# State-space stage of a four-layer kernel: spread products placed in opposite row halves of TensorE, sines stored 64 rows off, products of constants in front of three waits

## The reference, cut to what matters

```python
def _rope(t, theta):
    na = theta.shape[-1]                      # 32 angles
    x1, x2, rest = (t[..., :na], t[..., na:2 * na], t[..., 2 * na:])
    c, s = (jnp.cos(theta), jnp.sin(theta))
    return jnp.concatenate([x1 * c - x2 * s, x1 * s + x2 * c, rest], axis=-1)
...
theta = jnp.cumsum(angles[:, :, None, :] * dt[..., None], axis=1)
Bn = _rmsnorm(Bg, B_norm_w)
Cn = _rmsnorm(Cg, C_norm_w)
K = _rope(Bn[:, :, None, :] + B_bias, theta)
Q = _rope(Cn[:, :, None, :] + C_bias, theta)
...
S1 = jnp.einsum('bcihn,bcjhn->bcijh', Qc, Kc) * g1c[:, :, None, :, :] * decay
...
y = (y_intra + y_inter).reshape(b, L, NHEADS, HEADDIM)
y = y + D[None, None, :, None] * x
y = y * jax.nn.silu(z)
return y.reshape(b, L, D_INNER) @ W_out
```

## Time and profile before

| | us |
|---|---|
| median of 3 runs | 2860.07 |
| lowest and highest | 2855.85, 2862.87 |
| the profiled execution's own time | 2858.35 |
| its span, first to last instruction | 2856.4 |
| PE busy in the span | 2418.9 |
| DVE busy | 2147.7 |
| ACT busy | 1681.9 |
| POOL busy | 1036.5 |

### The profile page before, as it was taken

How to read it: one execution, slowest core, us unless ns; L and a number is a source line. 1 busy time by engine, 2 the same in 40 slices (tenths; PEclk the granted TensorE clock), 3 DMA queues, 4 the chain that set the end, 5 groups by cost and what they waited for, 6 DMA issues and landing times. The chain is left out here.

```text
span 2856.4 us, 37348 instructions
## 1 busy us (share of the span) xinstructions
PE 2418.9 (85%) x10635; PEld 1074.2 (38%) x10730; DVE 2147.7 (75%) x5906; ACT 1681.9 (59%) x3069; POOL 1036.5 (36%) x1019
## 2 busy tenths in 40 slices
PE   6666378787888999989999989989988888879998
PEld 2211266664353434343333333333341111234443
DVE  6999589995686665565666656678569999758886
ACT  3445344543655666662222258855569999877775
POOL 1333489994144554430000034400030000028886
PEclk8788566768989999999999999999999999999999
DMA  3112575624185656442111123300031111101110
GB/s 135 59 59 74 135 136 110 114 42 126 49 260 112 131 108 127 78 155 71 36 36 34 35 54 91 91 2 0 1 116 44 46 40 46 29 24 41 45 45 26
DMA packets 297804, 211.74 MB, mean 74 GB/s; under 512 B 157640, under 2 KB 262008, under 8 KB 296952
## 3 DMA queue, kind: packets, MB, share of 16 engines
q1 hardware_dynamic: 258992, 189.78, 24.9%
q0 software_dynamic: 20352, 17.05, 4.1%
q10 hardware_dynamic: 18256, 2.52, 0.6%
HBM read 136.24 MB, written 62.52 MB: 70 GB/s over the span
## 5 line engine op out<-in xcount | busy, mean ns | idle before, releaser
L3221 ACT ACTIVATE ca_pw<-ca_ps,ca_mx 128x512 f32<-128x512 f32 x512 | 342.7, 939 | 7.3 <-DVE ca_mx L3257 7.3
L3257 DVE TENSOR_REDUCE ca_mx<-ca_ps 128x1 f32<-128x512 f32 x512 | 311.1, 673 | 0.7 <-PE ca_ps L3187 0.7
L3053 DVE CUSTOM_DVE_ANT_0 mx_sums<-mx_ps,w_w2f 128x384 f32<-128x384 f32 (+3 forms) x512 | 218.1, 486 | 112.2 <-PE mx_ps L3008 110.7
L2996 PE MATMUL gm_ps<-gm_h,w_w2f 128*128 128x512 f32 x512 | 239.0, 607 | 3.1 <-DVE gm_h L3081 3.1
L3221 ACT ACTIVATION_READ_ACCUMULATOR ca_pw<-ca_ps,ca_mx 128x1 f32 x512 | 234.9, 459 | 0.0
L3187 PE MATMUL ca_ps<-qs,ks 128*128 128x512 bf16 x484 | 172.1, 395 | 55.7 <-ACT ca_pw L3221 41.7
L2695 ACT ACTIVATE ta_pw<-ta_ps,w_cst 128x1280 f32<-128x1280 f32 x128 | 168.0, 1322 | 35.4 <-PE ta_ps L2572 35.1
L3125 ACT ACTIVATE gm_h<-gm_ps,w_w2f 128x512 f32<-128x512 f32 x64 | 44.0, 687 | 218.4 <-PE gm_ps L2996 218.4
L2827 DVE TENSOR_TENSOR ta_pw<-ta_pw,w_cst 128x384 f32<-128x384 f32 x128 | 70.7, 552 | 133.6 <-ACT ta_pw L2695 131.0
L2418 ACT ACTIVATE at_pw<-at_ps 128x1280 f32<-128x1280 f32 x128 | 157.1, 1238 | 19.2 <-PE at_ps L2384 19.0
L2740 POOL DMA_INDIRECT Acc<-XN,f_idx x64 | 103.7, 1620 | 155.8 <-DVE XN L2798 141.2
(11 more groups left out here) (594 smaller groups left out, 6272.6 us busy)
## 6 DMA issues: line engine op xcount, KB each, us to landing
Pd<-s_p SPq DMA_DIRECT2D x48, 384.0 KB, 5.0
ex_w<-e_w SPq DMA_DIRECT2D x48, 256.0 KB
Qd<-rp_q SPq DMA_DIRECT2D x4, 2048.0 KB, 7.6
ss_ellb<-Rd SPq DMA_DIRECT2D x32, 256.0 KB, 3.3
qs<-Pd SPq DMA_DIRECT2D x32, 192.0 KB, 4.2
ks<-Pd SPq DMA_DIRECT2D x32, 192.0 KB, 4.6
Pd<-cs_p SPq DMA_DIRECT2D x16, 384.0 KB, 2.4
GX<-Qd SPq DMA_DIRECT2D x44, 128.0 KB
```

The costliest lines, as they stand in the source:

```text
L2996: last = pe.matmul(at, W(("h1", "h2")[layer])[:, j * 512 + f * 128:j * 512 + (f + 1) * 128], (h0, h1)[layer][:, j, :], start=(j == 0), sto ...
L3053: return v.tensor_tensor_reduce(out=sums[:, bank, at:at + n], in0=ps[:, bank, at:at + n], in1=K["w2f"]("down")[:, T - n:T], scale=-1.0, sc ...
L3221: act.activation(pw[:, h % BUF, jk, :], ps[:, (h * NB + jk) % BANKS, :], ACT.Exp, bias=mx[:, h % H, jk:jk + 1], accum_out=z[:, h % H, jk:j ...
L3257: v.tensor_reduce(mx[:, h % H, jk:jk + 1], ps[:, q % BANKS, :], AX.X, ALU.max, negate=True).then_inc(S["top"], 1)
```

## The change

Four edits, all in `ssm_phase` and its constants.

1. `spread(h)` uses only 64 of the 128 rows in each product, and the two products use opposite halves: the cosines of heads 0 and 1 lie in rows 0 to 63 and are multiplied there, the sines of the same heads in rows 64 to 127, and the other way round for heads 2 and 3.
2. For that the sines are stored 64 rows off: ScalarE makes them with two Sin operations of 64 partitions in place of one of 128, and `spread_sin` is rotated to match.
3. `means` has two products of constants in front of its wait for `sq` in every block after the first (the first keeps its four).
4. `products(1)` and `products(2)` have one product of constants, and their two waits change places: first `a[h-1]`, then the product of constants, then `turned[h]`.

```diff
             def means(i):
                 pe.wait_ge(HD["a"][H - 1], i)
-                if i == 0:
-                    kept_busy(pe, K, ps[:, 0, :], 4)
+                kept_busy(pe, K, ps[:, 0, :], 2 if i else 4)
                 pe.wait_ge(S["sq"], i + 1)
...
                     for n in range(2):
-                        last = pe.matmul(ps[:, 3 + n, :], cst(("spread", "spread_sin")[n])[:, h * 128:(h + 1) * 128],
-                                         th[:, 1 + n, :],
-                                         start=True, stop=True)
+                        half = slice(64 * ((h // 2 + n) % 2), 64 * ((h // 2 + n) % 2) + 64)
+                        last = pe.matmul(ps[:, 3 + n, :], cst(("spread", "spread_sin")[n])[half, h * 128:(h + 1) * 128],
+                                         th[half, 1 + n, :], start=True, stop=True)
                     last.then_inc(HD["cps"][h], 1)
...
                 def products(h):
-                    pe.wait_ge(HD["turned"][h], i + 1)
                     if h:
                         pe.wait_ge(HD["a"][h - 1], i + 1)
+                    if h in (1, 2):
+                        kept_busy(pe, K, ps[:, 0, :], 1)
+                    pe.wait_ge(HD["turned"][h], i + 1)
...
                 act.wait_ge(S["clamp"], i + 1)
-                act.activation(th[:, 2, :], th[:, 0, :], ACT.Sin).then_inc(S["sin"], 1)
+                act.activation(th[64:128, 2, :], th[0:64, 0, :], ACT.Sin)
+                act.activation(th[0:64, 2, :], th[64:128, 0, :], ACT.Sin).then_inc(S["sin"], 1)
                 act.activation(th[:, 1, :], th[:, 0, :], ACT.Abs).then_inc(S["abs"], 1)
...
-        "spread_sin": np.concatenate([((i[:, None] // 32 == h) & (i[None] < 64) & (i[:, None] % 32 == i[None] % 32))
+        "spread_sin": np.concatenate([(((i[:, None] + 64) % 128 // 32 == h) & (i[None] < 64) & (i[:, None] % 32 == i[None] % 32))
                                       * np.where(i[None] < 32, -1, 1).astype(np.float32) for h in range(4)], 1),
```

## The result

| | before | with the change |
|---|---|---|
| median us (6 runs each) | 2859.51 | 2871.52 |
| lowest to highest | 2855.85 to 2862.87 | 2869.31 to 2875.74 |
| ratio to before | | 1.0045, 95% interval 1.0034 to 1.0057 |
| profiled execution, own time | 2858.35 | 2875.74 |
| its span | 2856.4 | 2874.0 |

The kernel became 12.0 us slower, 0.4%. Forecast were +12.8 and 2873 us. The profiled execution with the change is the highest of its six runs, and its phase also begins 3.0 us later (first projection at 2545.43 in place of 2542.40); in the profiles of this study that start wanders between 2542 and 2556 us, by work ahead of the phase that no edit touches. So I compare the distances inside the phase. From the first projection to the last instruction the phase takes 328.6 us in place of 314.0.

The account below looks back on a forecast made before the run. The ssm_phase chain between engines was taken as the bound, TensorE busy 34.68 of 36.39 us a block. Seven steps of 1.72, 0.85 in the last block and -0.1 in block 0 gave +12.8, forecast 2873 us, range 2861 to 2880.

Parts of the forecast that it names:

- Part 1: Spread pairs: two 64-row products run side by side in 1.06 us, so products(0) starts 0.48 us earlier.
- Part 2: Constants in products(1) and products(2), behind the wait for a, overshoot the gaps; products(2) ends 0.85 us late.
- Part 3: Constants in front of means delay the means, so Ln and the next spread(0) come 1.72 us late.
- Part 4: Second Sin on ScalarE takes 0.52 us, upper bound a whole one, hidden by the constants in means except in block 0.
- The sum: Whole kernel: seven steps of 1.72, 0.85 in the last block, -0.1 in block 0, together +12.8 us.
- The last block: Last block of the phase, with no means behind it: 0.85 us late.
- there is no slower clock to be won back: TensorE in the kernel before: granted clock 1.00, the 2.4 GHz level, in the windows of all eight blocks.
- rival that the clock drops: TensorE drops to 1.2 GHz for part of the phase, 30 us for one block in eight, above 2885; chance 0.03.
- rival that the constants run inside the waits: TensorE's constants fill only waiting time, so not slower: -1.6 us, 2858.5 us; chance 0.1.

Follow-up runs that it names:

- e4: Pairs with both spread products in the same half, one Sin and no new constants, against the kernel before: 2875.08 us, ratio 1.0029.
- e7: The change with the constants of products(1) and products(2) moved ahead of the wait for a, into bank 7: 2868.64 us, ratio 1.0005 to before.
- e5: The change without the constants in means: 2874.42 us, ratio 1.0031 to the kernel before.
- e8: The kernel before with only the second Sin and rotated constants, full spreads, no new products of constants: 2872.51 us, ratio 1.0027.
- f0: The change itself, run again: 2879.19 us, ratio 1.0048 to the kernel before.
- e1: The change without its new products of constants, so pairs and two Sins only: 2881.47 us, ratio 1.0052 to the kernel before.
- f2: As f1, with one product of constants in means: 2862.74 us, ratio 0.9992 to the kernel before.
- e2: The constants alone, with full spreads and one unrotated Sin, against the kernel before: 2879.72 us, ratio 1.0049.
- e3: As e1 with the single Sin, so the turns are not the reference's: 2866.95 us, ratio 1.0002 to the kernel before.
- f3: As f1 without any new product of constants: 2865.53 us, ratio 1.0000 to the kernel before.
- f1: The change with one Sin shifted by VectorE copies, constants in products ahead of the wait for a, none in means: 2863.41 us, ratio 0.9994 to before.

## Why the prediction was right, and where it wasn't

**The pairs (Part 1): right.** 1.06 us for a pair, the next product 0.10 longer, `spread(1)` at `t2[0]`, `products(0)` 0.58 earlier in the block and ended 0.48 earlier. The rule of the Trainium skill on the drain (TensorEngine Tiling (Array Packing), Tiling Modes) stays at its small price: e4 shows 0.19 for the way in and out together.

**The constants in products (Part 2): right** in place and size. `products(2)` came 0.83 late (0.95 forecast) and ended 0.73 late (0.85). e7 shows the mechanism: moved ahead of the wait, in another bank, the same products delay `products(1)` by nothing.

**The constants in means (Part 3): right.** The means start 2.11 late in the block (2.07 forecast), and the block is 1.75 longer (1.72). Without them (e5) a block is only 0.34 shorter, as the second Sin then comes out from under them.

**The second Sin (Part 4): hidden, as said, but mis-sized.** "I take 0.52, by the same column count." From the first Sin to Abs it adds 0.77: the pace behind the two Sins is 0.64 and 0.65 in place of 0.52 for one. That is above what the prediction gave as the upper bound. In e8, uncovered, it cost 0.78 us a block in place of 0.33. In block 0, where nothing covers it, the way from the Sin to the Square grew by 0.78 (1.83 in place of 1.05). The sum came out near in spite of it because the constants in means hide the Sin in all seven steps.

**The last block: wrong by 1.45 us.** I had 0.85 for it. From `norm` to the end it took 41.07 in place of 38.77, 2.30 more, as the last outputs ran at the lower clock, 3.96 in place of 2.38. With the last outputs at full clock, e5, which has the same constants in `products`, took 39.47, 0.70 more. The slow last outputs came again in f0 (4.07), but also in e1, e8 and f2, and not in e2, e5 or e7: behind the same gap of 2.24 in every kernel, they go neither with the spreads nor with the constants, and what decides them is open. In all, the phase of the profile grew by 14.6 us: 0.83 to the first `norm`, 0.93 for the step out of block 0, six of 1.75, and 2.30. The sum had 12.8. The medians say 12.0 and 13.6.

**The clock: the right sentence for the sum, the wrong one for the change.** That "there is no slower clock to be won back" holds against the kernel before, and the change runs at 1.00 up to its last outputs. But the rival that the clock drops got 0.03 with "for it: nothing". Without the constants, the kernels with pairs do drop it: in seven of eight blocks of e1's profile, in one or two of those of e3 and f3. Its price was off as well: the rival took a whole block at the lower level, 30 us, and a fall at `products(2)` costs 4.2. With a product of constants in front, `products(2)` held its clock in all 48; so the change pays 12 to 14 us in both comparisons, where e1, without the constants, pays 15 by its ratio, and between 4.5 and 38 from run to run. The intervals of the two ratios overlap, so which of them is slower on the whole isn't shown. The rival that the constants run inside the waits promised 2858.5, 1.6 under before; with `products(2)` at full clock and the Sin avoided, f1's blocks show that such a gain is there, 0.4 us a block, and that it is small.

## What to carry to other kernels

A product of constants should stand ahead of the wait whose gap it is to fill, in a bank that is free then: behind the wait it delays what follows by its full length, and the same number moved ahead of it gave back 0.8 to 1.3 us a block. Price an edit that makes TensorE's work narrower or shorter by its gaps and its clock together, and test it with and without the products that keep it busy: neither half told what the whole would do. And where a stage is passed between engines, a delay can cost more than itself, since it moves operations under those of another engine: 1.66 us became 4.2 here.

## What was not expected of the hardware

- The granted clock fell at `products(2)` in some blocks of every kernel that has spreads of 64 rows and no constants in front of it, behind gaps of 1.54 us and once of 0.69 (e4), and in none of the 16 of the kernel before and e8, with spreads of 128 rows and gaps of 0.60 and 0.69. Whether the rows or the gaps matter wasn't separated: spreads of 128 rows with a gap of 1.54 in front of `products(2)` were not run.
- An activation over 64 partitions took 0.63 us, no less than one over 128, and its successor started 0.64 to 0.65 later in place of 0.52. Whether the other partitions of the output or the 64-row shape make it so was not tried.
- Five VectorE operations of 128x512 from SBUF to SBUF that took 3.4 us beside GpSimd's operations of 128x128 took 6.7 beside its operations of 128x512.
